# Score tiles in seven PSUM banks taken in pairs, and later layer norms cut into pieces on four engines

## The chip, the cores and the metric

One NeuronCore of a Trainium2 chip runs the whole program. Its engines are TensorE (PE in the profile), VectorE (DVE), ScalarE (ACT), GpSimd (POOL) and SyncE (SP, which here only issues DMAs). Each engine works through its own list of instructions in order and waits on semaphores. The metric is the device time of one execution, in microseconds.

## The reference

The input `x` is `[4, 1024, 128]` in float32. Four blocks follow each other, each added to its own input: a two-layer Mamba block; an encoder layer with a mixture-of-experts attention; then the two attentions that this case is about, and a switch feed-forward.

```python
# L1_attn: 16 heads of width 8, causal, rotary, a distance decay
q_rot, k_rot = _rotate(q, cos, sin), _rotate(k, cos, sin)
scores = einsum('bhqd,bhkd->bhqk', q_rot, k_rot) / sqrt(8) + decay_bias
attn = softmax(where(causal, scores, -inf)); out = (attn @ v) @ Wo.T
# L1_ffn: a second attention, not causal, then eight experts
hn = layernorm(x, ln1_g, ln1_b)
q, k, v = hn @ wq + bq, hn @ wk + bk, hn @ wv + bv      # 16 heads of width 8
x1 = x + (softmax(q @ k.T / sqrt(8)) @ v) @ wo + bo
hn2 = layernorm(x1, ln2_g, ln2_b)
y = x1 + w2[idx] @ relu(w1[idx] @ hn2 + b1[idx]) + b2[idx], idx = argmax(hn2 @ gate_w + gate_b)
```

`L1_attn` is applied to `layernorm(x)`, and `L1_ffn` to `layernorm` of its result, so a batch of the second attention needs two layer norms one after the other.

## The kernel before

The program has four phases with a barrier after each: `Mamba`, `SwitchHead`, `NarrowAttentions`, `MoeFfn`. The change is in the third.

**Sources and units.** A source is one batch of one attention: sources 0 to 3 are the causal attention's batches, 4 to 7 the other's (`NB` = 4). Each source makes two units of 8 heads, so there are 16 units, 0 to 7 causal and 8 to 15 not. Within a unit, `hp` is a pair of heads, `t` one of 8 tiles of 128 tokens and `q` one of two halves of 512 tokens.

**Steps.** For each (`hp`, `t`, `q`) a unit has a `row` and a `col`. A `row` step is two matmuls (one for each head, line 2253) into a pair of PSUM banks, and a maximum over them on VectorE (line 2418). A `col` step is two matmuls of the transposed scores (line 2271) into a pair of banks, with the row maximum already subtracted by three extra contraction rows, and one exp on ScalarE (line 2357) into the SBUF tile `P`. Causal tiles on the diagonal add masking matmuls (lines 2258, 2276). A `values` step multiplies one `t` of `P` with the values into the accumulator bank `OB` (line 2300). After 8 of these ScalarE copies the bank out (`copy`, line 2364), TensorE transposes it (`finish`, line 2227) and VectorE divides by the sums (lines 2438, 2445). When a unit's rows are done, `max_mm` and `max_t` bring the maxima into place through TensorE, ScalarE and six small DMAs. A causal unit has 48 rows and 48 cols, another 64 and 64.

**The order** is one list of steps, made by `order`, which every engine goes through and takes its own parts of. The rows of unit n+1 are dealt among the cols of unit n, nearly one for one; in the last unit there are only cols, and before unit 0 only rows. `after` adds `values`, `copy` and, two cols later, `finish`; `out_t` and `out` (the output projection, one per source) follow in the next unit. A side sequence `source(s)` prepares source s during unit 2s-3 (source 1 during unit 0's rows): one of its steps follows every third col. Its steps are `norm` (and `norm2` for s >= 4), `rows` (8 transposes, ScalarE copies them to `XT`), for each of two sides `qk`, (`qk2`), `hi`, `mid`, `lo`, and at last `v`. `experts_first` does the same for the first expert batch (`g_norm`, `g_rows`) in unit 15.

**The norms** are whole on VectorE (`layer_norm`): 8 bn_stats, 8 bn_aggr, a wait for ScalarE's square root (`row_root`, line 198, between two loads of an activation table), five small operations, 8 tensor_scalars (line 204), and with a gain two broadcast tensor_tensors (lines 2485, 2487).

**PSUM.** Banks 0 to 5 are a ring, `Banks(..., c.ps, 6, ...)`, in which every use takes 2 neighbouring banks; banks 6 and 7 are the two `OB`. A use waits on TensorE (`empty`) until the reader of the last use of its banks is done; the reader waits for `full`.

## Time and profile before

| | us |
|---|---|
| median of 3 runs (lowest, highest) | 6000.66 (5996.47, 6005.03) |
| the profiled execution: its own time | 6004.54 |
| its span in the profile | 6002.8 |
| the phase `NarrowAttentions` in it | 3948 to 5505 |
| unit 13 (not causal, no source beside it) | 95.2 |
| unit 9 (not causal, with source 6) | 121.8 |

A unit is read here from the copy of its predecessor's last `OB` to that of its own last `OB`. PE busy time counts pipelined matmuls and their modelled ends, so a busy PE can still be waiting for a bank.

### The profile page before, as it was taken

The page shows a single profiled execution, that of the slowest core. Times are in us where ns is not written, and L with a number is a line of the kernel's source. Part 1 is how long each engine was busy: PE and PEld are TensorE (multiplying, and loading weights), DVE is VectorE, ACT ScalarE, POOL GpSimd, SP SyncE. Part 2 cuts the span into 40 slices and gives each one's busy share as a digit, 9 for nine tenths or more (in the row PEclk, how much of TensorE's full clock was granted, in tenths as well). Part 3 has the DMA queues.
Part 4 walks back from the last instruction along what each step waited for, and adds up shares of the span by engine and source line. Part 5 has one row for each costly group of instructions (what it writes and reads, how often), then busy time and mean ns, then how long its engine had stood idle before and what let it go on. Part 6 is the DMA issues. An engine that isn't in the chain of part 4 may idle for free. (4 is left out here: it accounts for less than half of the span.)

```text
span 6002.8 us, 73017 instructions
## 1 busy us (share of the span) xinstructions
PE 5422.2 (90%) x25792; PEld 2257.1 (38%) x25792; DVE 4262.6 (71%) x4735; ACT 2550.3 (42%) x2902; POOL 2487.9 (41%) x1169
## 2 busy tenths in 40 slices
PE   7988987799999999999999999968888787887999
PEld 2333333233333334333433343333332222222777
DVE  6999898877777776777677767576667878871222
ACT  5655563232223233222332323225555666675332
POOL 4888887566555655556555556510000000000000
PEclk9999999899999999999999999979998999998999
DMA  4555554010101010101101100122111100101000
GB/s 148 187 183 185 181 190 160 20 41 20 35 21 31 20 41 23 31 20 37 27 20 34 40 20 26 35 47 39 36 28 28 28 22 22 23 1 30 4 4 8
DMA packets 133557, 314.62 MB, mean 52 GB/s; under 512 B 29644, under 2 KB 50516, under 8 KB 132916
## 3 DMA queue, kind: packets, MB, share of 16 engines
q1 hardware_dynamic: 133208, 309.96, 17.7%
q8 instruction: 220, 3.60, 0.2%
q14 instruction: 129, 1.06, 0.1%
HBM read 268.05 MB, written 23.86 MB: 49 GB/s over the span
## 5 line engine op out<-in xcount | busy, mean ns | idle before, releaser
L2418 DVE TENSOR_REDUCE n_MX<-ps 128x2 f32<-128x1024 f32 (+1 forms) x896 | 972.5, 1107 | 250.2 <-PE ps L2253 166.8
L1962 POOL TENSOR_TENSOR s_PA<-s_PA,shared 128x1024 f32<-128x1024 f32 x384 | 908.9, 2367 | 318.6 <-ACT shared L1538 290.7
L2357 ACT ACTIVATE n_P<-ps 128x1024 f32<-128x1024 f32 (+2 forms) x896 | 816.0, 932 | 448.2 <-PE ps L2271 227.3
L1538 ACT ACTIVATE shared<-ps 128x1024 f32<-128x1024 f32 x512 | 522.6, 1023 | 1127.3 <-PE ps L1372 1115.1
L766 POOL TENSOR_TENSOR m_PR<-m_HH,m_CS 128x1024 f32<-128x1024 f32 x256 | 606.0, 2383 | 162.1 <-issue 146.5
L1704 DVE TENSOR_REDUCE s_MX<-ps 128x2 f32<-128x1024 f32 x512 | 592.5, 1200 | 5.8 <-PE ps L1355 5.5
L1696 DVE TENSOR_TENSOR XTB<-ps,s_GVJ 128x1024 f32<-128x1024 f32 x256 | 312.8, 1222 | 358.4 <-PE ps L1346 356.4
L1355 PE MATMUL ps<-s_QF 64*128 64x512 f32 x2048 | 501.9, 607 | 71.2 <-DVE XTB L1696 44.8
L1368 PE MATMUL ps<-s_QF 64*128 64x512 f32 x2048 | 554.1, 617 | 6.6 <-DVE s_MX L1704 4.7
L2300 PE MATMUL ps<-n_P,n_VA 128*32 128x512 f32 (+3 forms) x3584 | 529.6, 590 | 18.7 <-ACT n_P L2357 18.3
L543 PE MATMUL ps<-m_PR,ident 128*128 128x512 f32 x1024 | 505.7, 621 | 11.1 <-DVE m_ZS L735 6.6
L1410 PE MATMUL ps<-s_OG,s_WO 128*128 128x512 f32 x1024 | 501.8, 612 | 0.7 <-DVE s_OUTT L1746 0.5
L1383 PE MATMUL ps<-shared,s_V 128*64 128x512 f32 x2048 | 499.0, 608 | 0.0
L1346 PE MATMUL ps<-s_WV,XTB 128*128 128x512 f32 x1024 | 482.8, 594 | 1.3 <-DVE XTB L1696 0.8
L729 DVE TENSOR_TENSOR_SCAN m_HH<-m_DA,ps 128x1024 f32<-128x1024 f32 x176 | 402.4, 2286 | 6.6 <-ACT m_DA L665 0.6
L1733 DVE TENSOR_TENSOR s_OG<-ps,s_OT 128x1024 f32<-128x1024 f32 x256 | 310.8, 1214 | 90.8 <-issue 61.1
L1924 POOL TENSOR_TENSOR s_TA<-s_TA,s_CS 128x1024 f32<-128x1024 f32 x64 | 151.3, 2365 | 475.4 <-DMA s_TA<-XTB 475.4
L2496 POOL TENSOR_TENSOR XTB<-XTB,n_PT 128x1024 f32<-128x1024 f32 x14 | 29.8, 2132 | 719.0 <-ACT n_PT L2330 708.7
L1698 DVE TENSOR_REDUCE s_V<-XTB 128x128 f32<-128x1024 f32 x256 | 312.3, 1220 | 8.8
L1355 PEld LDWEIGHTS ps<-s_QF 64*128 64x128 f32 x2048 | 200.9, 190 | 304.2 <-issue 274.5
L1410 PEld LDWEIGHTS ps<-s_OG,s_WO 128*128 128x128 f32 x1024 | 178.1, 189 | 307.9 <-issue 306.3
L1368 PEld LDWEIGHTS ps<-s_QF 64*128 64x128 f32 x2048 | 177.2, 186 | 290.4 <-issue 284.8
(344 smaller groups left out, 7816.2 us busy)
## 6 DMA issues: line engine op xcount, KB each, us to landing
m_CS<-m_rows_c SPq DMA_DIRECT2D x256, 512.0 KB, 3.7
m_BS<-m_rows_c SPq DMA_DIRECT2D x80, 512.0 KB, 5.0
s_WV<-in_s_v SPq DMA_DIRECT2D x32, 512.0 KB, 3.6
s_TA<-XTB SPq DMA_DIRECT2D x256, 64.0 KB, 2.3
s_WO<-in_s_o SPq DMA_DIRECT2D x32, 512.0 KB, 4.0
n_parts<-n_PT SPq DMA_DIRECT2D x14, 768.0 KB, 3.3
shared<-n_parts SPq DMA_DIRECT2D x144, 64.0 KB
n_QS<-n_parts SPq DMA_DIRECT2D x120, 64.0 KB
```

The costliest lines, as they stand in the source:

```text
L543: ins = pe.matmul(self.PY[:, q], c.ident[:, :], self.PR[n % 4][:, q], start=j == 0, stop=j == self.NS - 1)
L766: g.tensor_tensor(self.PR[n % 4][:, :], self.HH[n % 4][:, :], self.CS[n % self.NCS][:, :], ALU.mult).then_inc(self.prod_done, 1)
L1355: ins = pe.matmul(ps[:, 512 * h:512 * h + 512], QF[hs, 0, t * 128:(t + 1) * 128], QF[hs, 1, 512 * q:512 * q + 512], start=True, stop=True)
L1368: pe.matmul(ps[:, 512 * h:512 * h + 512], QF[hs, 1, t * 128:(t + 1) * 128], QF[hs, 0, qs], start=True, stop=False)
L1383: ins = pe.matmul(self.O[64 * h:64 * h + 64, :], self.V[j % 2][:, h, t, :], self.P[g % 4][:, 512 * h:512 * h + 512], start=t == 0, stop=t ...
L1410: ins = pe.matmul(self.Z, self.WO[j % 2][:, 2 * e + i, :], self.OG[e % 2][:, i, :], start=e == i == 0, stop=e == 3 and i == 1)
L1538: s.activation(self.P[g % 4], ps, ACT.Exp).then_inc(*r.take(step))
L1704: v.tensor_reduce(self.MX[:, q, :, t], ps.rearrange("p (h n) -> p h n", h=2), AX.X, ALU.max, negate=True).then_inc(*r.take(step))
L1962: g.tensor_tensor(PA, PA, P, ALU.add).then_inc(self.add_done, 1)
L2300: ins = pe.matmul(ob[at:at + 32, lo - 512 * q:512], self.VA[s % 3][:, t, 8 * g + 2 * hp + hh, :], self.P[(32 * n + 8 * hp + t) % 3][q][:, ...
L2357: s.activation(self.P[(32 * n + 8 * hp + t) % 3][q][:, :, lo:512], ps.rearrange("p (h n) -> p h n", h=2)[:, :, lo:512], ACT.Exp, scale=sca ...
L2418: v.tensor_reduce(self.MX[:, q, :, hp, t], ps.rearrange("p (h n) -> p h n", h=2)[:, :, 0:width], AX.X, ALU.max).then_inc(*r.take(step))
```

## The change

A new class `Pairs` replaces `Banks` for this phase: it has seven banks, and use k takes the next two, going round, so that one use in seven has bank 6 and bank 0. A use that needs one access pattern over both (`apart` false: all but `row` and `col`) skips bank 6 instead. A `row` or `col` on the pair (6, 0) is read by two instructions, one for each bank. One bank, 7, is left for `OB`.

The norms become four steps: `norm` (the statistics, VectorE), `norm_root` (ScalarE), `norm_scale` (six small operations, VectorE) and `norm_out` (8 activations, ScalarE). The gain after `norm2` and `g_norm` is a step of its own on GpSimd, and so is the last bias of `out` for sources 4 to 7. Each step still follows a third col, or a second one in units 5 and 7. Left out of the diff: renamed semaphores, an unchanged copy of `Banks`' methods, and that the steps' counts follow.

```diff
+class Pairs:
+    def __init__(self, nc, ctx, name, PS, n, uses):
+        self.full = ctx.enter_context(nc.semaphore(f"{name}_full"))
+        self.read = {e: ctx.enter_context(nc.semaphore(f"{name}_read_{e}")) for e in "vs"}
+        self.q, self.place, self.before, self.reader, self.turn = {}, {}, {}, {}, {}
+        at, count, seen = 0, {"v": 0, "s": 0}, [{"v": 0, "s": 0} for _ in range(n)]
+        banks = PS[:, 0:512 * n].rearrange("p (b n) -> p b n", b=n)
+        for k, (step, apart, reader) in enumerate(uses):
+            if at == n - 1 and not apart:
+                at = 0
+            two = sorted((at, (at + 1) % n))
+            mine = [seen[b] for b in two]
+            self.before[step] = {e: max(m[e] for m in mine) for e in "vs"}
+            count[reader] += 1
+            for m in mine:
+                m[reader] = count[reader]
+            if not apart:
+                self.q[step] = PS[:, 512 * at:512 * at + 1024]
+            elif two[1] - two[0] == 1:
+                self.q[step] = [banks[:, two[0]:two[0] + 2, :]]
+            else:
+                self.q[step] = [banks[:, b:b + 1, :] for b in two]
+            self.place[step], self.reader[step], self.turn[step] = k + 1, reader, count[reader]
+            at = (at + 2) % n
+    def half(self, step, h):
+        return self.q[step][0][:, h, :] if len(self.q[step]) == 1 else self.q[step][h][:, 0, :]
...
-        self.OB = [c.ps[:, 3072:3584], c.ps[:, 3584:4096]]
+        self.OB = c.ps[:, 3584:4096]
-        self.r = Banks(nc, ctx, "n_psum", c.ps, 6, [(s, 2, who(s)) for s in self.steps if s[0] in engine or s[0] == "qk"])
+        self.r = Pairs(nc, ctx, "n_psum", c.ps, 7, [(s, s[0] in ("row", "col"), who(s)) for s in self.steps if s[0] in engine or s[0] == "qk"])
...
     def source(self, s):
         out = self.out
-        out.append(("norm", s))
-        yield
+        yield from self.norm_pieces("norm", s)
         if s >= NB:
-            out.append(("norm2", s))
+            yield from self.norm_pieces("norm2", s)
+            out.append(("gain", s))
             yield
...
     def experts_first(self):
-        for kind in ("g_norm", "g_rows"):
+        yield from self.norm_pieces("g_norm", 0)
+        for kind in ("g_gain", "g_rows"):
             self.out.append((kind, 0))
             yield
+    def norm_pieces(self, kind, s):
+        for k in (kind, kind + "_root", kind + "_scale", kind + "_out"):
+            self.out.append((k, s))
+            yield
...
-            cols = list(self.cols(n))
+            cols, apart = list(self.cols(n)), 2 if n < 8 and s >= NB else 3
-                if i % 3 == 2:
+                if i % apart == apart - 1:
...
-                pe.wait_ge(self.norm_done, n)
+                if n < NB:
+                    pe.wait_ge(self.ln_out, self.ln("norm", n))
+                else:
+                    pe.wait_ge(self.gain_done, n - NB + 1)
...
-            if 4 * n + hp >= 2:
-                pe.wait_ge(self.oc_done, 4 * n + hp - 1)
+            if 4 * n + hp > 0:
+                pe.wait_ge(self.oc_done, 4 * n + hp)
...
-                s.activation(self.P[(32 * n + 8 * hp + t) % 3][q][:, :, lo:512], ps.rearrange("p (h n) -> p h n", h=2)[:, :, lo:512],
-                             ACT.Exp, scale=scale).then_inc(*r.take(step))
+                P, at = self.P[(32 * n + 8 * hp + t) % 3][q], 0
+                for x in ps:
+                    ins = s.activation(P[:, at:at + x.shape[1], lo:512], x[:, :, lo:512], ACT.Exp, scale=scale)
+                    at += x.shape[1]
+                ins.then_inc(*r.take(step))
...
             if kind in ("norm", "norm2", "g_norm"):
-                self.layer_norm(v, own, step)
+                if self.ln(*step) > 1:
+                    v.wait_ge(self.ln_out, self.ln(*step) - 1)
+                if kind == "g_norm":
+                    v.wait_ge(self.y_done, 1)
+                stats_sums(c, v, own, self.norm_source(kind, n), self.norm[step])
+            elif kind in ("norm_scale", "norm2_scale", "g_norm_scale"):
+                stats_scale(c, v, own, self.norm[kind[:-6], n], (self.ln_chain, 1))
...
-                v.tensor_reduce(self.MX[:, q, :, hp, t], ps.rearrange("p (h n) -> p h n", h=2)[:, :, 0:width], AX.X,
-                                ALU.max).then_inc(*r.take(step))
+                at = 0
+                for x in ps:
+                    ins = v.tensor_reduce(self.MX[:, q, at:at + x.shape[1], hp, t], x[:, :, 0:width], AX.X, ALU.max)
+                    at += x.shape[1]
+                ins.then_inc(*r.take(step))
...
-                r.taken(v, step)
-                if n >= NB:
-                    v.tensor_tensor(dst, dst, self.lnp[:, 3, :].unsqueeze(1).to_broadcast([128, NT, 128]),
-                                    ALU.add).then_inc(self.y_done, 1)
...
+    def norm_out(self, s, kind, n):
+        c, r = self.c, self.r
+        src = self.norm_source(kind, n)
+        dst = self.norm_source("norm2", n) if kind == "norm" and n >= NB else self.XN
+        s.wait_ge(self.ln_chain, self.ln(kind, n))
+        if kind == "norm" and n == NB + 1:
+            s.wait_ge(self.va0_done, 1)
+        elif kind == "norm" and n == NB + 2:
+            for side in range(2):
+                r.taken(s, ("qk", NB - 1, side))
+                r.taken(s, ("qk2", NB - 1, side))
+        if dst is self.XN:
+            before = self.S if kind == "g_norm" else n
+            if before > 1:
+                r.filled(s, ("rows", before - 1))
+        for i in range(NT):
+            ins = s.activation(dst[:, i, :], src[:, i, :], ACT.Identity, scale=c.rs[:, 6, i:i + 1],
+                               bias=c.rs[:, 7, i:i + 1])
+        ins.then_inc(self.ln_out, 1)
...
+            if kind in ("gain", "g_gain"):
+                XN, t = self.XN[:, :, :], self.lnp if kind == "gain" else self.glnp
+                g.wait_ge(self.ln_out, self.ln("norm2" if kind == "gain" else "g_norm", n))
+                g.wait_ge(self.consts_in, 16 * 4)
+                g.tensor_tensor(XN, XN, row(t, 0), ALU.mult).then_inc(*own.up())
+                own.wait()
+                g.tensor_tensor(XN, XN, row(t, 1), ALU.add).then_inc(self.gain_done, 1)
+            elif kind == "out" and n >= NB:
+                dst = c.Y[:, (n - NB) * NT:(n - NB + 1) * NT, :]
+                r.taken(g, step)
+                g.tensor_tensor(dst, dst, row(self.lnp, 3), ALU.add).then_inc(self.y_done, 1)
```

## Rows read from the trace of the kernel before

**Rows 1.** Page, busy time and share of the span of one engine

```profile
PE 5422.2 (90%) x25792; PEld 2257.1 (38%) x25792; DVE 4262.6 (71%) x4735; ACT 2550.3 (42%) x2902; POOL 2487.9 (41%) x1169
```

**Rows 2.** Windows (stretch, length; PE, PEld, DVE, ACT, POOL busy; clock): phase, units 6, 9, 13

```profile
3948.00:5500.00 1552.00, 1245.14 (x9920) 418.50 (x9920) 1136.07 (x1651) 960.81 (x1125) 84.96 (x40) 0.91 0.13 26
4502.18:4575.15 72.97, 65.60 (x651) 25.54 (x649) 52.47 (x68) 42.65 (x58) 0.00 (x0) 0.95 0.14 24
4778.35:4900.11 121.76, 88.91 (x563) 24.86 (x561) 94.86 (x153) 81.04 (x88) 8.55 (x4) 0.89 0.11 27
5221.25:5316.47 95.22, 78.35 (x531) 19.41 (x529) 79.69 (x83) 67.10 (x72) 0.00 (x0) 0.95 0.10 18
```

**Rows 3.** Timeline, one round of the steady pattern, unit 12: start, us, engine, line

```profile
5165.27 0.39 PE L2271 MATMUL ps<-shared 51*128 51x512 bf16 x2
5165.70 3.00 ACT L2357 ACTIVATE n_P<-ps 128x1024 f32<-128x1024 f32 x3 [0.51 <-PE ps L2271]
...
5166.86 0.39 PE L2253 MATMUL ps<-n_KS,n_QS 48*128 48x512 bf16 x2 [0.77 <-ACT n_P L2357]
...
5167.30 3.68 DVE L2418 TENSOR_REDUCE n_MX<-ps 128x2 f32<-128x1024 f32 x3 [0.16 <-PE ps L2253]
...
5168.10 1.06 PE L2300 MATMUL ps<-n_P,n_VA 128*32 128x512 f32 x8
...
5169.53 1.02 ACT L2357 ACTIVATE n_P<-ps 128x1024 f32<-128x1024 f32 x1 [0.83 <-PE ps L2271]
...
5170.64 0.39 PE L2271 MATMUL ps<-shared 51*128 51x512 bf16 x2
```

**Rows 4.** Groups of instructions by form: exps, and maxima of units 5 to 14

```profile
L2357 ACT ACTIVATE n_P<-ps 128x1024 f32<-128x1024 f32 x704 | 702.0, 1023 | 288.3 <-PE ps L2271 227.3 <-PE ps L2276 52.9
L2357 ACT ACTIVATE n_P<-ps 128x512 f32<-128x512 f32 x64 | 38.2, 598 | 70.3 <-PE ps L2276 70.3
...
L2418 DVE TENSOR_REDUCE n_MX<-ps 128x2 f32<-128x512 f32 x12 | 8.3, 693 | 5.5 <-PE ps L2258 5.2
```

**Rows 5.** Timeline, the norms of source 6 in unit 9

```profile
4782.72 1.64 DVE L176 BATCH_NORM_STATS2 ln_stats<-X 128x6 f32<-128x128 f32 x8
4783.05 1.28 ACT L198 ACT_TABLE_LOAD   x1
...
4786.56 2.14 DVE L204 TENSOR_SCALAR Y<-X,ln_mean_var,ln_small 128x128 f32<-128x128 f32 x8
...
4792.27 1.63 DVE L176 BATCH_NORM_STATS2 ln_stats<-Y 128x6 f32<-128x128 f32 x8
...
4799.34 1.23 DVE L2485 TENSOR_TENSOR n_XN<-n_XN,n_lnp 128x1024 f32<-128x1024 f32 x1
...
4803.06 0.61 PE L2271 MATMUL ps<-shared 51*128 51x512 bf16 x2 [7.74 <-DVE n_MX L2418]
```

**Rows 6.** Windows: first quarters of units 9 and 13, and 4 us after a stall

```profile
4778.35:4822.90 44.55, 27.13 (x152) 7.73 (x150) 35.12 (x84) 26.24 (x27) 2.14 (x1) 0.77 0.20 35
5221.25:5247.93 26.68, 22.08 (x140) 5.22 (x138) 21.91 (x22) 17.61 (x18) 0.00 (x0) 0.87 0.34 58
...
4790.00:4794.00 4.00, 3.94 (x18) 0.74 (x18) 3.92 (x11) 1.48 (x2) 0.00 (x0) 0.50 0.55 98
```

**Rows 7.** Timeline of VectorE: first and last of nine maxima beside ScalarE's parts

```profile
4839.37 1.23 DVE L2418 TENSOR_REDUCE n_MX<-ps 128x2 f32<-128x1024 f32 x1 [0.31 <-PE ps L2253]
...
4851.37 1.23 DVE L2418 TENSOR_REDUCE n_MX<-ps 128x2 f32<-128x1024 f32 x1 [0.31 <-PE ps L2253]
```

**Rows 8.** Timeline, ScalarE's scale-and-bias activations in the phase before

```profile
3944.64 1.65 ACT L1482 ACTIVATE s_XN<-s_XN,ln_small 128x128 f32<-128x128 f32 x4 [2.91 <-DVE ln_small L810]
```

**Rows 9.** Page, the costliest groups: a GpSimd tensor_tensor on float32

```profile
L1962 POOL TENSOR_TENSOR s_PA<-s_PA,shared 128x1024 f32<-128x1024 f32 x384 | 908.9, 2367 | 318.6 <-ACT shared L1538 290.7
```

**Rows 10.** Timeline, the norm of source 1, ahead of unit 0

```profile
3956.53 2.50 DVE L189 TENSOR_SCALAR ln_small<-ln_small 128x8 f32<-128x8 f32 x1
...
3962.50 1.94 PE L2190 MATMUL ps<-ident,n_XN 128*128 128x128 f32 x8 [8.97 <-DVE n_MX L2418]
```

More of the change, by code:

```diff
@@ L86, in __init__, with ap, empty, filled @@
             at += width
+    def ap(self, step):
+        return self.q[step]
+    def empty(self, e, step):
+        for reader, count in self.before[step].items():
+            if count:
+                e.wait_ge(self.read[reader], count)
+    def filled(self, e, step):
+        e.wait_ge(self.full, self.place[step])
+    def taken(self, e, step):
+        e.wait_ge(self.read[self.reader[step]], self.turn[step])
+    def fill(self, step):
+        return self.full, 1
+    def take(self, step):
+        return self.read[self.reader[step]], 1
+class Pairs:
[24 more added lines that the diff above has]
+        return self.q[step][0][:, h, :] if len(self.q[step]) == 1 else self.q[step][h][:, 0, :]
     def ap(self, step):
@@ L2252, in row @@
             hs = slice(64 * hh, 64 * hh + k)
-            ins = pe.matmul(ps[:, 512 * hh:512 * hh + width], Q[hs, hp, t * 128:(t + 1) * 128],
+            ins = pe.matmul(self.r.half(step, hh)[:, 0:width], Q[hs, hp, t * 128:(t + 1) * 128],
                             K[hs, hp, 512 * q:512 * q + width], start=True, stop=not diag)
@@ L2256, in row @@
             for hh in range(2):
-                hs, end = slice(64 * hh, 64 * hh + 64), 512 * hh + width
-                ins = pe.matmul(ps[:, end - 128:end], self.EM[hs, a, :], self.EM[hs, 2 + a, :], start=False, stop=a == 1)
+                hs = slice(64 * hh, 64 * hh + 64)
+                ins = pe.matmul(self.r.half(step, hh)[:, width - 128:width], self.EM[hs, a, :], self.EM[hs, 2 + a, :], start=False, stop=a == 1)
         ins.then_inc(*self.r.fill(step))
@@ L2270, in col @@
             hs = slice(64 * hh, 64 * hh + k)
-            ins = pe.matmul(ps[:, 512 * hh + lo - 512 * q:512 * hh + 512], K[hs, hp, t * 128:(t + 1) * 128],
+            ins = pe.matmul(self.r.half(step, hh)[:, lo - 512 * q:512], K[hs, hp, t * 128:(t + 1) * 128],
                             Q[hs, hp, lo:512 * q + 512], start=True, stop=not diag)
@@ L2274, in col @@
             for hh in range(2):
-                hs, at = slice(64 * hh, 64 * hh + 64), 512 * hh + lo - 512 * q
-                ins = pe.matmul(ps[:, at:at + 128], self.EM[hs, a, :], self.EM[hs, 4 + a, :], start=False, stop=a == 1)
+                hs, at = slice(64 * hh, 64 * hh + 64), lo - 512 * q
+                ins = pe.matmul(self.r.half(step, hh)[:, at:at + 128], self.EM[hs, a, :], self.EM[hs, 4 + a, :], start=False, stop=a == 1)
         ins.then_inc(*self.r.fill(step))
@@ L2309, in scalar @@
             ps = r.ap(step) if step in r.q else None
-            if kind in ("norm", "norm2", "g_norm"):
-                row_root(c, s, self.norm[step])
+            if kind in ("norm_root", "norm2_root", "g_norm_root"):
+                row_root(c, s, self.norm[kind[:-5], n])
+            elif kind in ("norm_out", "norm2_out", "g_norm_out"):
+                self.norm_out(s, kind[:-4], n)
             elif kind in ("rows", "g_rows"):
@@ L2451, in vector @@
                 v.tensor_tensor(flat(dst), flat(dst), ps, ALU.add).then_inc(*r.take(step))
-                r.taken(v, step)
-                if n >= NB:
-                    v.tensor_tensor(dst, dst, self.lnp[:, 3, :].unsqueeze(1).to_broadcast([128, NT, 128]),
-                                    ALU.add).then_inc(self.y_done, 1)
         c.own_count = own.n
-    def layer_norm(self, v, own, step):
-        c, n = self.c, step[1]
-        if step[0] == "norm" and n < NB:
-            if n > 1:
-                self.r.filled(v, ("rows", n - 1))
-            row_stats(c, v, own, c.batch(n), self.norm[step])
-            normalize(c, v, own, c.batch(n), self.XN, (self.norm_done, 1))
-            return
-        first = step[0] == "g_norm"
-        Yb = c.Y[:, 0:NT, :] if first else c.Y[:, (n - NB) * NT:(n - NB + 1) * NT, :]
-        if first:
-            v.wait_ge(self.y_done, 1)
-        if step[0] == "norm":
-            if n == NB + 2:
-                for side in range(2):
-                    self.r.taken(v, ("qk", NB - 1, side))
-                    self.r.taken(v, ("qk2", NB - 1, side))
-            row_stats(c, v, own, c.batch(n - NB), self.norm[step])
-            normalize(c, v, own, c.batch(n - NB), Yb)
-            own.wait()
-            return
-        v.wait_ge(self.consts_in, 16 * 4)
-        gain = lambda i: (self.glnp if first else self.lnp)[:, i, :].unsqueeze(1).to_broadcast([128, NT, 128])
-        row_stats(c, v, own, Yb, self.norm[step])
-        self.r.filled(v, ("rows", self.S - 1 if first else n - 1))
-        normalize(c, v, own, Yb, self.XN)
-        own.wait()
-        v.tensor_tensor(self.XN[:, :, :], self.XN[:, :, :], gain(0), ALU.mult).then_inc(*own.up())
-        own.wait()
-        v.tensor_tensor(self.XN[:, :, :], self.XN[:, :, :], gain(1), ALU.add).then_inc(self.norm_done, 1)
@@ new lines, in norm_source @@
+    def norm_source(self, kind, n):
+        return self.c.batch(n % NB) if kind == "norm" else self.c.Y[:, n % NB * NT:(n % NB + 1) * NT, :]
+    def norm_out(self, s, kind, n):
[17 more added lines that the diff above has]
+        ins.then_inc(self.ln_out, 1)
@@ L2502, in gpsimd @@
     def gpsimd(self, g):
-        r = self.r
+        c, r = self.c, self.r
+        own = Own(g, self.own_gain)
+        row = lambda t, i: t[:, i, :].unsqueeze(1).to_broadcast([128, NT, 128])
         for u in range(3):
```

18 lines of the change are left out of this document (11 added, 7 removed).

## The prediction

> **What bounds the kernel now.** The page comes first: TensorE is busy for 90% of the span [rows 1]. The change touches only the third phase, 1557 us of it, so the windows come next. There no engine is full: TensorE 80%, VectorE 73%, ScalarE 62% [rows 2]. Such a phase is bound by a loop of waits, and the timeline shows which. In the steady pattern of a non-causal unit a round of 4 rows, 4 cols and 2 values steps takes 5.37 us [rows 3]: a col is filled at 5165.27, its exp starts at 5165.70, the next exp follows back to back and ends at about 5167.7; that frees the banks of the row at 5167.78; the values step starts at 5168.10, then a col, a row and a second values step, and the next round's col fills at 5170.64. Two exps and two values steps in series are the loop. VectorE is beside it with 4 x 1.227 = 4.9 us of work, ScalarE with 4.0 us and gaps of 0.51 and 0.83.
>
> The ring closes this loop: it has 3 slots, so use k waits for the reader of use k-3; the row at 5166.86 waited 0.77 us for an exp [rows 3]. Anything put on VectorE or ScalarE stops the others within three uses. Unit 9 with its source takes 121.8 us, unit 13 without one 95.2 [rows 2]. The first quarters show where: 44.55 against 26.68, so 17.9 us go in the quarter with both norms [rows 6]. VectorE is blocked there from 4782.72 to 4788.70 and from 4792.27 to 4801.8, 6.0 and 9.5 us [rows 5]; TensorE idles for up to 7.7 us, and the granted clock after the first stall is 0.50, the lower level, 1.2 GHz [rows 6].
>
> **Seven banks.** I go through the ring's rule use by use. With pairs (0,1) (2,3) (4,5) (6,0) (1,2) (3,4) (5,6), use k always holds one bank of use k-3, and the other is of k-3 or k-4. `empty` waits for both before the first matmul, so the wait is for use k-3, as with six banks; a skipped bank 6 leads to the same. Over the list's 1923 uses I count no steady use that could start a use earlier. The gain is 0: the seventh bank holds half a tile that nobody can start on. If I were wrong and a row or col could start one use earlier, the loop would open until VectorE bounds it at 1.23 a row in place of 1.34; that is a rival below.
>
> What it costs: 143 rows and 123 cols fall on (6,0) and are read by two instructions. A maximum over half the width takes 0.693 [rows 4], so two take 1.39 against 1.23: +0.16 each, 22 us of VectorE in all. Two exps of 0.598 take 1.20 against 1.023 [rows 4]: +0.17 alone; three full ones in a row take 3.00 and not 3.07 [rows 3], so I take 0.14, 17 us of ScalarE. Of this VectorE's part mostly fits in its 0.47 us of idle time a round; it counts ahead of unit 0, where only rows run: 7 x 0.16 = 1. Of the exps two in four are in the loop: 8. Sum +9; bounds 4 and 39. The Trainium skill (ScalarE: Activation LUTs, What ACT_TABLE_LOAD costs) has back-to-back activations overlap by 93 ns, twice or more what these rows show; by it a wrapped col costs 0.08 and the term is 6.
>
> One `OB`: values of t = 0 now wait for the copy just before. In the list `finish`, which waits on TensorE for that same copy, stands ahead of that values step for every head pair. It is the cover, and the cost is 0. Without it each of 63 copies would add up to its 0.6 us.
>
> **Norms in pieces: the price of a piece.** ScalarE's gaps let me work out what an insertion of X costs the loop: before the second exp of a back-to-back pair all of X, before the others X - 1.1 or nothing. The mean for 1.05 us is 0.53. The trace tests it: 8 intervals of maxima beside two such pieces take 12.00 us [rows 7] against 8 x 1.34 = 10.8, so 0.6 for each. On VectorE I let an insertion lose 0.8 (its idle 0.47 a round and the lead of its readers; between 0.5 and 1.1). By this the two blocks cost 15.5 - 1.6 = 13.9, the lower clock some 2, and 2 are left of the 17.9 for transposes and copies, which fits.
>
> Before, for a norm with its stall: VectorE 6.0 (statistics 2.5, wait and small operations 1.35, normalize 2.14), with ScalarE's root hidden in it. After, four insertions:
> - statistics, VectorE 2.5: costs 1.7
> - root, ScalarE, table load 1.28 [rows 5], sqrt 0.2, load back 1.28, together 2.77, now with nothing beside it that waits anyway: (2.77 + 1.67)/2 = 2.2
> - scale, VectorE, five small operations and a sixth, 1.2: 0.4
> - out, ScalarE: four such activations take 1.65 [rows 8], so 8 take 3.3, against VectorE's 2.14 for the same: (3.3 + 2.2)/2 = 2.75
>
> Together 7.05, 14.1 for two norms. The gain's two tensor_tensors (1.23 each [rows 5]) leave VectorE for GpSimd, 2 x 2.37 [rows 9]. `rows` waits for them on TensorE, with all later steps behind it; but six cols, over 8 us, lie between `norm2_out` and `rows`, against 3.3 + 4.75 from ScalarE's start. In units 5 and 7 only four do, and I count 1.4 us of stall for each.
>
> **The sum**, against the profiled 6004.5:
> - wrapped pairs +9
> - sources 6 and 7: 14.1 + 0.5 of clock against 13.9 + 2: -1.3, taken -1.5 each; sources 4 and 5, in causal units with more idle time (VectorE 72% in unit 6 [rows 2]), -1 each with the stall: together -5
> - sources 2 and 3: one norm, 7.05 less the causal slack against 5.2 and half a clock fall: 0
> - source 1: only rows run, so the exposed work is VectorE's. TensorE idled 8.97 [rows 10]; 8.8 of VectorE become 4.3, and `rows` waits some 1.5 for ScalarE: -3
> - the first expert norm, in unit 15 where ScalarE is the bound: about 8 us lost before, and 2.77 + 3.3 + a copy of 1.02 and 1 us of waiting for GpSimd after: 0
> - three biases of `out` leave VectorE: 3 x -1.2 = -3.5; the fourth is the phase's last work, 1.23 becomes 2.37 and a semaphore: +1.3
>
> Sum: 9 - 5 - 3 - 3.5 + 1.3 = -1.2, so 6003.3 for the profiled execution. It stands 3.9 above the median of the runs, so the forecast is 5999. For this kernel 0.2% is 12 us; less can't be told from no change.
>
> **Rivals.**
> - *Faster: pieces hide.* If every ScalarE piece costs half its length, as 1.05 us did [rows 7], a norm costs 3.0 + 2.1 = 5.1. Four sources give 10.2 - 15.9 = -5.7 each, sources 2 and 3 -1 each: 25 us in all with the other terms, 5976. For it: the two pieces that cost 0.6 each. Against it: the pieces are three times as long as the gaps. 0.24.
> - *Faster: the seventh bank opens the loop.* 512 non-causal pairs x 0.11 = 56 us, 5945. The wait for k-3 speaks against it. 0.03.
> - *Slower: the second instruction of a wrapped pair is in the path every time.* Place: each use of (6,0). Price: 22 + 17 = 39 in place of 9, so 6029. For it: every reader frees a slot that someone waits for within three uses; against it, the two loop exps of four. It decides once more than 22 of the 39 us are exposed. 0.17.
> - *Slower: no piece is absorbed.* A norm costs 3.7 + 6.07 = 9.8; against the blocks at full length this is +18 over the forecast, 6017. 0.08.
> - *Slower: GpSimd holds VectorE up.* A tensor_scalar on 8 columns took 2.50 us while GpSimd's memset ran, against 0.17 elsewhere [rows 10]; 14 new GpSimd operations x 2.37 would be 33 us, 6032. Maxima of PSUM beside GpSimd work kept their 1.23, so only a small operation can be caught. 0.03. The Trainium skill (SBUF — State Buffer, Who interferes with whom) says the same of both kinds: the port pair is locked for a whole instruction, and a tensor_reduce never asks for it. The trace agrees with its 2.50 and 1.23.
> - *The forecast:* 0.45, by itself 5989 to 6013.
>
> Range: from the hidden pieces to most of the wrapped pairs' price, 5975 to 6025. Faster 0.27, within 0.2% 0.45, slower 0.28.
>
> **What would show it.** Quarters of unit 13, with no source: 22.19 before; 22.3 to 22.5 if the ring gains nothing and the wraps cost half, 22.7 and more if all, under 21.5 if the loop opened. TensorE's wait of 0.77 on an exp must still be in the steady round. Unit 9's first two quarters: the pieces as four stalls of 1.5 to 3 us in place of two of 5.5 and 7.7, and a clock above 0.77. ScalarE's total rises by 12 x 3.3 + 17 = 57 us; VectorE's falls by 12 x 2.14 + 14 x 1.23 - 22 - 2 = 19. GpSimd's rises by 33. The forecast is wrong if units without a source move by more than 1 us, or if unit 9 moves by more than 4.

## The result, and the profile after

The changed kernel is slower by 0.3%: its median is 6019.99 us (7 runs, 6017.60 to 6025.88) against 6001.19 for the kernel before in the same sitting (7 runs, 5996.47 to 6006.16), a ratio of 1.0031 [1.0021, 1.0041]. The forecast was 5999 and no measurable change. The profiled execution of the changed kernel took 6025.88 with a span of 6024.1.

The page's line of busy time, to be read against [rows 1]:

```profile
PE 5443.6 (90%) x25754; PEld 2258.0 (37%) x25792; DVE 4235.6 (70%) x4782; ACT 2590.1 (43%) x3122; POOL 2520.1 (42%) x1183
```

VectorE lost 27 us of work, ScalarE gained 40, GpSimd 32: the work moved about as the diff says, and all of it was done. The time is lost elsewhere. The windows of the same stretches as in [rows 2]: the phase, then units 6, 9, 13.

```profile
3948.00:5513.76 1565.76, 1264.09 (x9908) 417.30 (x9908) 1109.52 (x1696) 1000.75 (x1344) 115.46 (x53) 0.91 0.12 26
4499.56:4572.23 72.67, 64.87 (x683) 26.71 (x683) 51.86 (x78) 43.91 (x66) 0.00 (x0) 0.99 0.11 24
4782.53:4913.46 130.93, 99.19 (x563) 25.49 (x561) 89.54 (x144) 87.32 (x115) 13.23 (x6) 0.83 0.10 25
5238.34:5333.90 95.56, 78.64 (x533) 19.44 (x529) 80.34 (x93) 67.51 (x81) 0.00 (x0) 0.95 0.12 18
```

Units 6 and 13, beside which no source is prepared, are where they were (72.97 and 95.22 before). Unit 9, with source 6, went from 121.76 to 130.93, though VectorE has 5.3 us less to do in it; ScalarE has 6.3 more and the granted clock fell from 0.89 to 0.83. All units, in us from copy to copy (unit 0 from 3948):

| unit | 0 | 1 | 2 | 3 | 4 | 5 | 6 | 7 |
|---|---|---|---|---|---|---|---|---|
| before | 145.8 | 84.8 | 71.7 | 85.9 | 71.7 | 94.4 | 73.0 | 108.2 |
| after | 142.5 | 91.3 | 72.1 | 91.4 | 72.2 | 96.2 | 72.7 | 101.0 |

| unit | 8 | 9 | 10 | 11 | 12 | 13 | 14 | 15 |
|---|---|---|---|---|---|---|---|---|
| before | 95.0 | 121.8 | 101.9 | 121.6 | 97.7 | 95.2 | 97.6 | 82.6 |
| after | 95.3 | 130.9 | 96.5 | 132.2 | 96.5 | 95.6 | 96.5 | 83.1 |

The last accumulator is copied at 5496.57 before and at 5513.76 after, so 17.2 of the two spans' 21.3 us arise in these units. Units 9, 11, 1 and 3 lose 9.2, 10.7, 6.5 and 5.5; units 7, 10 and 0 win 7.2, 5.4 and 3.3. Of the other 4 us, 1.2 is the last bias, now 2.34 on GpSimd; 2.9 lie in the last phase, which the change doesn't touch.

Where in unit 9? Its four quarters, each from one copy of `OB` to the next:

```profile
4782.53:4818.78 36.25, 24.85 (x140) 5.66 (x138) 27.75 (x64) 23.38 (x33) 0.00 (x0) 0.78 0.24 43
4818.78:4852.47 33.69, 25.91 (x146) 6.58 (x144) 20.58 (x27) 24.52 (x34) 4.72 (x2) 0.84 0.00 0
4852.47:4881.10 28.63, 23.79 (x138) 6.15 (x137) 19.85 (x22) 21.13 (x27) 5.21 (x3) 0.88 0.07 28
4881.10:4913.46 32.36, 24.64 (x145) 7.10 (x145) 21.36 (x33) 18.29 (x23) 3.31 (x2) 0.84 0.08 28
```

Before they took 44.55 [rows 6], 28.59, 24.49 and 24.13. The first two quarters, which hold both norms, together win 3.2 us. The third loses 4.1 and the last 8.2, and no piece of a norm runs in the last. The timeline of the last quarter shows what does:

```profile
4884.54 2.12 POOL L2575 TENSOR_TENSOR XTB<-XTB,n_PT 128x1024 f32<-128x1024 f32 x1 [2.25 <-ACT n_PT L2404]
4885.26 1.49 DVE L2510 TENSOR_TENSOR n_MM<-n_MX 128x64 f32<-128x64 f32 x1
...
4886.80 0.30 PE L2287 MATMUL ps<-ident,n_MM 128*64 128x128 f32 x1 [2.22 <-DVE n_MM L2510]
...
4889.11 1.93 PE L2369 MATMUL ps<-n_P,n_VA 128*32 128x512 f32 x8
...
4897.42 2.36 PE L2279 MATMUL ps<-n_wf,XTB 128*128 128x128 f32 x16
4897.53 1.02 ACT L2430 ACTIVATE n_P<-ps 128x1024 f32<-128x1024 f32 x1 [2.21 <-PE ps L2340]
...
4899.82 1.68 DVE L2491 TENSOR_TENSOR n_VA<-ps,n_lnp 128x128 f32<-128x128 f32 x8 [3.47 <-PE ps L2279]
```

The source's last steps (the residues on GpSimd at line 2575, that is, what is left of `XTB` when a bf16 piece is taken off, and the matmuls and additions of `v` at 2279 and 2491) now fall together with `max_mm` and `max_t` of the next unit (2510, 2287). The source has 19 steps in place of 12, still one after every third col, so it ends behind col 57 of the unit's 64 and not behind col 36. After the 2.22 us in which TensorE waited, a values step takes 1.93 in place of 1.06: the clock is at its lower level, 1.2 GHz, again.

The pieces in the first quarter look as the prediction drew them, with both table loads between exps and TensorE waiting behind them:

```profile
4793.84 1.28 ACT L253 ACT_TABLE_LOAD   x1
...
4795.14 0.21 ACT L253 ACTIVATE ln_small<-ln_small 128x8 f32<-128x8 f32 x1
4795.36 1.28 ACT L2430 ACT_TABLE_LOAD   x1
4796.65 1.94 ACT L2430 ACTIVATE n_P<-ps 128x1024 f32<-128x1024 f32 x2
4797.82 0.61 PE L2322 MATMUL ps<-n_KS,n_QS 48*128 48x512 bf16 x2 [2.65 <-ACT n_P L2430]
...
4806.20 3.18 ACT L2560 ACTIVATE Y<-X,ln_small 128x128 f32<-128x128 f32 x8
```

And the steady round of unit 12, against [rows 3]: the row still waits 0.77 for an exp, and a wrapped col is two instructions of 1.09 together.

```profile
5185.41 1.09 ACT L2430 ACTIVATE n_P<-ps 128x512 f32<-128x512 f32 x2 [0.84 <-PE ps L2340]
...
5186.95 3.00 ACT L2430 ACTIVATE n_P<-ps 128x1024 f32<-128x1024 f32 x3 [0.45 <-PE ps L2340]
...
5188.11 0.39 PE L2322 MATMUL ps<-n_KS,n_QS 48*128 48x512 bf16 x2 [0.77 <-ACT n_P L2430]
```

### The profile page after: what moved, and what is told of

The parts are those of the page before. It is cut to its first block and busy times, and to the rows that moved or that the text cites. A ratio compares the mean times of both kernels' runs of the same rounds, so it can differ in the third digit from the quotient of the medians.

```text
span 6024.1 us, 73273 instructions
## 1 busy us (share of the span) xinstructions
PE 5443.6 (90%) x25754; PEld 2258.0 (37%) x25792; DVE 4235.6 (70%) x4782; ACT 2590.1 (43%) x3122; POOL 2520.1 (42%) x1183
## 5 line engine op out<-in xcount | busy, mean ns | idle before, releaser
L2502 DVE TENSOR_REDUCE n_MX<-ps 128x2 f32<-128x1024 f32 (+7 forms) x1041 | 981.2, 974 | 289.5 <-PE ps L2322 187.9
L2430 ACT ACTIVATE n_P<-ps 128x1024 f32<-128x1024 f32 (+3 forms) x1020 | 821.2, 839 | 434.5 <-PE ps L2340 230.1
L2369 PE MATMUL ps<-n_P,n_VA 128*32 128x512 f32 (+3 forms) x3584 | 545.0, 608 | 20.6 <-ACT n_P L2430 20.4
L784 DVE TENSOR_TENSOR_SCAN m_HH<-m_DA,ps 128x1024 f32<-128x1024 f32 x176 | 402.5, 2287 | 6.6 <-ACT m_DA L720 0.6
L2322 PE MATMUL ps<-n_KS,n_QS 48*128 48x512 bf16 (+2 forms) x1120 | 215.7, 378 | 86.6 <-ACT n_P L2430 64.2
```

Source lines behind the costliest of these rows:

```text
L2369: ins = pe.matmul(ob[at:at + 32, lo - 512 * q:512], self.VA[s % 3][:, t, 8 * g + 2 * hp + hh, :], self.P[(32 * n + 8 * hp + t) % 3][q][:, ...
L2430: ins = s.activation(P[:, at:at + x.shape[1], lo:512], x[:, :, lo:512], ACT.Exp, scale=scale)
L2502: ins = v.tensor_reduce(self.MX[:, q, at:at + x.shape[1], hp, t], x[:, :, 0:width], AX.X, ALU.max)
```

## The experiments

All kernels are the changed one with these switches (for the kernel before, every part is switched back):

```diff
+RING, OBN = 7, 1      # banks of the ring, accumulator banks
+SPREAD = {...}        # norms cut into pieces; the others' parts stand together in the order, as before
+OUT_S = SPREAD        # norms whose 8 scale-and-bias operations run on ScalarE
+GAIN_G = {4, 5, 6, 7, 0}; BIAS_G = {4, 5, 6, 7}      # gains, last biases on GpSimd
+LATE_APART = 3        # cols from one side step to the next in units 9 and 11
```

| kernel | median | ratio to before | unit 9 | unit 11 | units 1, 3 |
|---|---|---|---|---|---|
| before | | | 121.8 | 121.6 | 84.8, 85.9 |
| after | 6019.99 | 1.0031 [1.0021, 1.0041] | 130.9 | 132.2 | 91.3, 91.4 |
| r7_only | 6009.32 | 1.0007 [0.9999, 1.0016] | 119.6 | 119.6 | 86.7, 85.4 |
| r7_halves | 6027.88 | 1.0043 [1.0029, 1.0057] | 124.2 | 122.3 | 87.3, 87.2 |
| norms_only | 6010.76 | 1.0018 [1.0009, 1.0026] | 130.7 | 132.5 | 91.1, 89.0 |
| gains_only | 5981.50 | 0.9967 [0.9955, 0.9979] | 120.6 | 120.0 | 84.8, 86.0 |
| norms_warm | 6019.38 | 1.0028 [1.0020, 1.0037] | 128.3 | 126.6 | 91.1, 88.9 |
| gains_warm | 5990.63 | 0.9980 [0.9971, 0.9989] | 124.4 | 120.1 | 84.9, 86.0 |
| spread_v | 6010.54 | 1.0012 [1.0003, 1.0021] | 127.7 | 129.1 | 88.9, 90.4 |
| whole_s | 6007.55 | 1.0005 [0.9997, 1.0014] | 121.0 | 124.1 | 86.7, 88.4 |
| norms_noload | 5985.94 | 0.9972 [0.9961, 0.9982] | 119.0 | 119.3 | 89.3, 88.0 |
| gains_noload | 5987.27 | 0.9974 [0.9965, 0.9983] | 120.6 | 118.6 | 84.8, 85.0 |
| norms_early | 5983.11 | 0.9967 [0.9955, 0.9980] | 118.8 | 118.0 | 91.1, 88.9 |
| after_early | 5995.33 | 0.9986 [0.9977, 0.9995] | 118.9 | 118.6 | 91.3, 91.4 |
| gains_late | 5992.61 | 0.9982 [0.9973, 0.9991] | 121.5 | 124.3 | 86.1, 84.9 |
| early_all | 6000.56 | 0.9993 [0.9985, 1.0002] | 119.0 | 118.8 | 95.6, 95.6 |
| mix | 5980.52 | 0.9964 [0.9950, 0.9978] | 123.1 | 120.0 | 86.0, 84.9 |
| early_best | 5983.85 | 0.9967 [0.9955, 0.9979] | 118.8 | 118.7 | 86.0, 84.9 |

### The ring alone, and the norms alone

**r7_only**: seven banks and one `OB`, all norms, gains and biases as before.

```diff
-SPREAD, GAIN_G, BIAS_G = {...}, {4, 5, 6, 7, 0}, {4, 5, 6, 7}
+SPREAD, GAIN_G, BIAS_G = set(), set(), set()
```

> The change's seven-bank pairs and single OB alone, with the norms whole on VectorE as before. Theory A (the ring gains no depth; the wrapped pairs' second instruction costs 0.3 to 0.5 us in a unit): slower than before by 3 to 8 us, quarters without a source 22.3 us against 22.19, and most of the change's 19 us lies elsewhere. Theory B (the wrapped pairs are the loss): slower by 15 us or more. If the ring did gain depth: faster, quarters under 22.

**norms_only**: the change without its ring.

```diff
-RING, OBN = 7, 1
+RING, OBN = 6, 1
```

> The change's norms, gains and biases with a ring of six banks (bank 6 unused, single OB). Theory A: slower than before by 11 to 16 us, units 9 and 11 each by 8 to 11, units 1 and 3 by 5 to 6, unit 7 and the stretch ahead of unit 0 shorter by 7 and 3. Theory B: within 4 us of before.

**gains_only**: of the change, only the gains and the last biases on GpSimd.

```diff
-RING, OBN, SPREAD = 7, 1, {...}
+RING, OBN, SPREAD = 6, 2, set()
```

> Before, with only the gains of norm2 and g_norm and the last bias of out moved to GpSimd; norms whole on VectorE, six banks, two OB. If what GpSimd takes is off VectorE's block and hidden by the cols ahead of rows: faster than before by 8 to 16 us. If rows now waits for GpSimd (4.7 us in place of 2.5, with only three cols between norm2 and rows): no faster than 3 us, with TensorE waiting at the transposes.

By its ratio r7_only loses some 4 us to the ring and the single `OB`, with an interval from nothing to 10. Two pairs of kernels differ in the ring alone: norms_only and the changed kernel, and norms_early and after_early (below). By their ratios the ring costs 8 and 11 us there, each give or take 8 or 9; all three readings together allow 4 as well as 10. A quarter of unit 13 with nothing beside it takes 22.19 with six banks and 22.25 to 22.32 with seven: no depth is gained, and little is paid. In units 9 and 11 the loss stays with the norms: norms_only has them as long as the changed kernel to 0.3 us. Moving the gains and biases alone wins 0.33%, some 20 us, more than was expected and more than the 14 instructions of 1.23 us that leave VectorE; of it 4.0 us are in unit 13, in whose code nothing is changed. There the clock goes with it; its first quarter and whole, in gains_only, against [rows 6] and [rows 2]:

```profile
5203.48:5227.41 23.93, 19.33 (x140) 5.11 (x138) 21.82 (x22) 17.60 (x18) 0.00 (x0) 1.00 0.31 66
5203.48:5294.72 91.24, 74.10 (x531) 19.44 (x529) 79.42 (x83) 66.82 (x72) 0.00 (x0) 1.00 0.09 19
```

VectorE's and ScalarE's work are the same to 0.3 us; the clock is 1.00 in place of 0.95. So the same unit is 91.2 or 95.2 long as the clock stands in it, above all behind the unit boundary, where 2.75 of the 4.0 us are, and differences of 4 us in a unit without a source prove nothing about its code. Unit 0, whose code is the same in the changed kernel and in after_early, took 142.5 and 137.4.

**r7_halves**: r7_only, where each of a pair's two matmuls waits for its own bank, the earlier free one first. It tests whether the odd bank can be used at all.

```diff
-        self.r.empty(pe, step)
-        for hh in range(2):
+        for hh in self.r.order(step):
+            self.r.empty_half(pe, step, hh)
```

> As r7_only, but row and col wait for each bank by itself, the earlier free one first, so that the seventh bank lets one of the two matmuls start a use earlier. If TensorE's fill were what the ring waits for: undisturbed quarters under 22.0 us against 22.25 and 22.32 in r7_only. My theory (the other matmul still waits for the reader of use k-3, and the reader needs both): 22.1 to 22.6, no faster.

It is slower by 0.4%; quarters without a source take 22.7 to 24.4. A first half that is written earlier helps nobody, since the reader waits for both. Why it is slower than r7_only no run separates.

### The clock

Both kernels add matmuls that nobody reads, into the bank that six banks and one `OB` leave free, to keep TensorE at work where it would wait for a norm. **norms_warm** is norms_only with 9 of them behind the statistics, the root and the output of each norm of sources 4 to 7; **gains_warm** is gains_only with one `OB` and 20 behind each statistics step of these sources.

```diff
+            if kind == "warm":
+                for _ in range(WARM):
+                    pe.matmul(c.ps[:, 3072:3584], self.EM[0:64, 0, :], self.EM[0:64, 0:4, :], start=True, stop=True)
```

> As norms_only, and TensorE multiplies nine times a constant tile of 512 columns into the unused bank 6 (results not read) three scores after the statistics, the root and the output of each norm of sources 4 to 7, to fill the stalls. Clock theory (each of the eight stalls per source drops TensorE to the 1.2 GHz level for some 3 us, and the values steps at 1.9 instead of 1.06 us are the loss): values steps at 1.06 in unit 9, granted clock above 0.92 there, and units 9 and 11 shorter than in norms_only by 3 to 6 us each. Serial theory (the pieces' own lengths on ScalarE are the loss, the clock is a by-product): the same or longer than norms_only, by up to 2 us for each source.

> As gains_only with one OB, and TensorE multiplies twenty times a constant tile of 512 columns into the unused bank 6 (results not read) three scores after each of the two statistics of sources 4 to 7, which fills most of the 5.5 us stalls. Clock theory: the values steps after the stalls take 1.06 and not 1.9 us, units 9 and 11 shorter by 2 to 4 us each than in gains_only. Serial theory: within 1 us.

In norms_warm the clock of units 9 and 11 rose from 0.83 and 0.82 to 0.89 and 0.91, and they took 2.3 and 5.9 us less; units 5 and 7 took 5.1 and 4.0 more, and the whole was slower. In gains_warm units 7 and 9 took 2.8 and 3.8 more than in gains_only, units 5 and 11 the same to 0.4. The clock carries a part of the loss, but this remedy costs as much as it gives, and how large the part is stays open.

### Which part of a norm costs when it is spread

**spread_v**: all norms in pieces, their eight scale-and-bias operations on VectorE.

```diff
-RING, OBN = 7, 1
+RING, OBN = 6, 2
 SPREAD = {...}
-OUT_S = SPREAD
+OUT_S = set()
```

> As gains_only, but each norm in four pieces with cols between, normalize still on VectorE. Serial theory (a piece stops the ring for about its own length, so what spreading costs is the root's 2.77 us, which VectorE's block hid before): units 9 and 11 at 125 to 127 us against 120 in gains_only and 131 in norms_only, unit 1 at 88 to 90 against 85. Rival (the loss is ScalarE's slower normalize, 3.2 for 2.1 us): units 9 and 11 at 119 to 122.

**whole_s**: gains_only, with the eight operations on ScalarE, all parts of a norm still together.

```diff
-OUT_S = set()
+OUT_S = {("norm", s) for s in range(1, 8)} | {("g_norm", 0)}
```

> As gains_only, each norm's steps together, but normalize on ScalarE. Serial theory: statistics to scale 3.9 us on VectorE and then 3.2 on ScalarE, 1.1 more than VectorE's 6.0 for each norm: units 9 and 11 at 121 to 124. Rival (ScalarE's part is most of the loss): 127 or more.

**norms_noload** and **gains_noload**: norms_only and gains_only, where a copy stands for the square root, so that no table is loaded.

```diff
-                row_root(c, s, self.norm[kind[:-5], n])
+                s.wait_ge(c.var_done, self.norm[kind[:-5], n])
+                s.activation(c.rs[:, 1, :], c.rs[:, 0, :], ACT.Copy).then_inc(c.root_done, 1)
```

> As norms_only, but the root of each norm of the third phase is a copy on ScalarE in place of the square root (so the output is not the reference's), and both table loads go. Serial theory: with the pieces spread, the 2.6 us of table loads stop the ring for their length: units 9 and 11 shorter than in norms_only (131 and 133) by 5 to 8 us each with the clock, unit 1 by 2 to 3. Rival (what spreading costs is the number of stalls, not their length): 1 to 3 us each.

> As gains_only, with the same copy in place of the square root (the output is not the reference's). Serial theory: VectorE's block hides the table loads but for its wait of 0.3 and 1.3 us, so units 9 and 11 are shorter than in gains_only (120.6 and 120.0) by 1 to 3 us each only. Rival: as much as in norms_noload, 5 us or more.

Putting the eight operations on VectorE wins 3 us in each of units 9 and 11, and 7 to 9 of the loss remain. In one piece whole_s adds 0.4 and 4.1 there. So the place of the eight operations is not what makes units 9 and 11 long. Over the whole it is not cheap, though: whole_s has lost all that gains_only had won, by the ratios some 23 us, of which units 1, 3, 5, 7 and 11 show 1.9, 2.4, 3.8, 4.7 and 4.1 (and unit 13, whose code it doesn't touch, 4.8). The table loads are a stronger term. Spread out, they are worth 11.7 and 13.2 us in units 9 and 11, more than the 4 x 1.28 of their own time; in one piece they are worth 0 and 1.4. The timeline of gains_only shows why that is so little: the load runs while VectorE computes the statistics, and the root waits only 0.94.

```profile
4777.45 1.63 DVE L843 BATCH_NORM_STATS2 ln_stats<-X 128x6 f32<-128x128 f32 x8
...
4777.78 1.28 ACT L253 ACT_TABLE_LOAD   x1
...
4780.00 0.21 ACT L253 ACTIVATE ln_small<-ln_small 128x8 f32<-128x8 f32 x1 [0.94 <-DVE ln_small L848]
```

But in units 1 and 3 the loads are worth only 1.9 and 1.0 of the 6.4 and 3.1 that spreading costs there, and in unit 9 they pay in quarters in which there is no load: its last falls from 32.36 to 29.2. The loads are an amplifier; something else makes the last quarter long. Yet without them units 9 and 11 are back at 119.0 and 119.3, though the source still ends behind col 57 and the last quarter is still long: taking out the loads wins as much as the late end costs.

### How far apart the side steps stand

**after_early**: the changed kernel, whole, but for one number: in units 9 and 11 a side step follows every second col, so the source ends behind col 38 and not 57. **norms_early** is norms_only with the same number.

```diff
-LATE_APART = 3
+LATE_APART = 2
```

> The changed kernel itself, ring of seven and all, with one number changed: in units 9 and 11 a side step follows every second col and not every third. If the late end of the source beside max_mm and max_t is what the change lost: last quarters at 23 to 25 us in place of 32.4, units 9 and 11 at 118 to 122, in all 18 to 28 us faster than the change and 3 to 10 faster than before. If the seven banks matter for it: still slower than before.

> As norms_only, but in units 9 and 11 too a side step follows every second col, so that a source ends at col 38 and not at col 57 of 64. If part of the loss is that hi, mid, lo and v of the second side now fall together with max_mm and max_t in the last quarter (32.4 us there against 24.1): the last quarter back at 24, units 9 and 11 shorter by 4 us or more. If it only moves the same stalls: within 2 us of norms_only, the last quarter shorter and the others longer.

In after_early this takes 12.1 and 13.6 us out of units 9 and 11 of the changed kernel and turns its ratio from 1.0031 to 0.9986. Unit 9 as a whole, then its first and its last quarter:

```profile
4777.45:4896.32 118.87, 90.99 (x563) 24.85 (x561) 88.40 (x147) 87.20 (x114) 13.24 (x6) 0.90 0.11 28
4777.45:4813.28 35.83, 23.92 (x140) 5.45 (x136) 28.55 (x70) 28.92 (x44) 0.73 (x1) 0.86 0.23 44
...
4873.34:4896.32 22.98, 17.84 (x129) 4.88 (x128) 18.35 (x24) 16.56 (x24) 0.00 (x0) 1.00 0.02 4
```

VectorE's and ScalarE's work in the unit is within 1.2 us of that in the changed kernel. The last quarter is 22.98 where it was 32.36, at full clock; GpSimd is idle in it. The norms' own first quarter did not grow (35.83 against 36.25).

**gains_late** makes the coincidence without the pieces: gains_only with a side step after every fifth col of units 9 and 11, so that the source ends behind col 60.

```diff
-LATE_APART = 3
+LATE_APART = 5
```

> As gains_only, with whole norms on VectorE, but in units 9 and 11 a side step follows every fifth col, so that the same twelve steps end at col 59 of 64. If the coincidence with the unit's end is a cost of its own, without any piece: last quarters at 30 us or more against 25.1, units 9 and 11 longer than 120.6 and 120.0 by 4 to 9 us. If the pieces are the cost: within 2 us.

The last quarters grow from 25.1 to 27.3 and 28.2, units 9 and 11 by 0.9 and 4.3, and the whole by some 9 us. The lateness alone costs, but a third or less of what it costs beside the pieces. (A last quarter of 30 us or more was expected.) The same quarter of unit 9 before, in gains_late and in norms_noload, to be read against the 32.36 at a clock of 0.84 above:

```profile
4875.98:4900.11 24.13, 19.29 (x129) 4.71 (x128) 18.41 (x22) 16.61 (x21) 0.00 (x0) 0.93 0.02 4
...
4867.79:4895.08 27.29, 21.71 (x145) 6.59 (x144) 20.25 (x30) 18.42 (x22) 2.12 (x1) 0.94 0.09 32
...
4859.23:4888.43 29.20, 21.55 (x145) 6.70 (x144) 21.17 (x30) 18.39 (x22) 3.25 (x2) 0.94 0.09 31
```

At a like clock a late source makes it 3.2 us longer, and 1.9 more where the norms are in pieces. norms_noload has the wait of 2.2 us for `n_MM` too; the last 3.2 us, from 29.20 to 32.36, come with the lower clock. These kernels differ in more than one thing, so this is a reading of the 8.2 us and not a proof.

One difference is to be seen in the steps themselves, `n_MM` of all 16 units, first in the changed kernel, then in gains_only:

```profile
L2510 DVE TENSOR_TENSOR n_MM<-n_MX x16: 224/226/1927, 4010.7 to 5425.0; 128x64 f32<-128x64 f32 x16
```

```profile
L2561 DVE TENSOR_TENSOR n_MM<-n_MX x16: 224/225/226, 4014.2 to 5385.5; 128x64 f32<-128x64 f32 x16
```

In the changed kernel it takes 1.49 in units 9 and 11, 1.93 in unit 5, 0.48 in units 1 and 3, and 0.22 elsewhere; in gains_late 0.58 at most. The long ones run beside GpSimd's residue, as in the timeline above, and `max_mm` is at the head of the chain on which all cols of the next unit wait. In units 1 and 3 the residue catches the next link of this chain, in `max_t`, which takes 0.27 elsewhere:

```profile
4158.19 1.81 DVE L2513 TENSOR_TENSOR n_MR<-n_MT,n_M 64x128 f32<-64x128 f32 x1 [0.41 <-ACT n_M L2416]
```

How much of a unit such an instruction makes, no run isolates. It need not be dear: in unit 5 of norms_only `n_MM` takes 1.87 and the unit 91.7, and in gains_only 0.22 and 91.1.

**early_all** is norms_early with a side step after every second col in units 1 and 3 too.

```diff
-... apart = ..., 2 if n < 8 and s >= NB and ("norm", s) in SPREAD else 3 if n < 8 or n == 15 else LATE_APART
+... apart = ..., 2 if n < 8 and s >= NB and ("norm", s) in SPREAD else 3 if n == 15 else LATE_APART
```

> As norms_early, with every second col in units 1 and 3 as well, where a source of 14 steps ended at col 42 of 48. If the same cause made units 1 and 3 slower (91.1 and 88.9 against 84.8 and 85.9 before): 84 to 87 there. If in those units the pieces themselves cost: still 88 or more.

Units 1 and 3 get worse, 95.6 against 91.1 and 88.9. Unit 1 by quarters: norms_only has 25.7, 22.6, 24.3 and 18.6, early_all 35.0, 23.8, 21.8 and 15.0. The end is freed here as well, by 6.1 us, and `n_MM` and `n_MR` of these units take 0.22 and 0.27 again, but the first quarter, into which the whole norm now falls together with the transposes, pays 9.3. In the causal units with one norm neither spacing wins against the block (84.8 and 85.9).

### Versions put together

**mix**: gains_only, with sources 1 and 5 in pieces and the last bias back on VectorE. **early_best**: sources 1 and 4 to 7 and the expert norm in pieces, side steps after every second col in units 5, 7, 9 and 11, sources 2 and 3 whole on VectorE, the expert norm's eight operations and the last bias on VectorE.

```diff
-RING, OBN, SPREAD, BIAS_G = 7, 1, {("norm", s) for s in range(1, 8)} | {("g_norm", 0)}, {4, 5, 6, 7}
+RING, OBN, SPREAD, BIAS_G = 6, 2, {("norm", 1), ("norm", 4), ("norm", 5), ("norm", 6), ("norm", 7), ("g_norm", 0)}, {4, 5, 6}
-LATE_APART = 3
+LATE_APART = 2
```

> As gains_only, with source 1 (only rows run beside it) and source 5 (in unit 7, 64 rows against 48 cols, VectorE 92 of 108 us busy, ScalarE 56) in four pieces with ScalarE's normalize, and the last bias back on VectorE. If pieces pay only where VectorE alone is the bound: the stretch ahead of unit 0 shorter by 8 to 10 us, unit 7 by 2 to 4, the rest as gains_only, in all 10 to 14 us faster than it. If the gain of unit 0 in norms_only was luck of the clock: within 4 us of gains_only.

> What the runs point to: six banks and two OB; source 1 and sources 4 to 7 in pieces, every second col in units 5, 7, 9 and 11; sources 2 and 3 whole on VectorE; the first expert norm in pieces with normalize on VectorE; gains on GpSimd, the phase's last bias on VectorE. By the sum of the best units seen (139 + 85 + 72 + 86 + 71 + 92 + 71 + 102 + 95 + 119 + 96 + 118 + 95 + 93 + 96 + 81) the phase ends near 5459 against 5476 in gains_only: 35 us faster than before, 20 to 40 with the clock's luck.

Both beat both kernels, and neither can be told from gains_only or norms_early: 0.9964 to 0.9967 with intervals of 0.0012 to 0.0014 to either side. Both expectations were too high: the sum of the best units seen gave 35 us for early_best, and 20 came. The simplest of them moves 14 instructions to GpSimd and changes nothing else. Beside that the pieces, well spaced, win 1.4 to 2.0 us in each of units 9 and 11 (after_early and norms_early against gains_only), less than a unit moves with the clock.

## Why the prediction was wrong

**The step that failed** is in "Norms in pieces: the price of a piece", with the term "sources 6 and 7: ... taken -1.5 each". It priced each piece where it stands and never asked what the seven added steps do to the steps behind them. That "each step still follows a third col" was in the description of the change; 19 steps of 3 cols end at col 57, and `max_mm` and `max_t` come just there. The two units were +9.2 and +10.7. With the one number of after_early they are -2.9 and -2.9 against before, of which the gains alone make -1.2 and -1.6 (gains_only). So in these two units the pieces' own price, as a sum, was about right, and it is the displacement that costs 12 to 14 us in each. That is shown for pieces with their table loads in them. It is not a cause by itself: without the loads the same late end leaves the units at 119.0 and 119.3, and without the pieces it costs 0.9 and 4.3. How the loss divides between the stretched `n_MM`, the lower clock and the plain overlap is read from unlike kernels above and not shown.

The terms of the sum against the units, in us:

| term | predicted | measured |
|---|---|---|
| wrapped pairs, all units | +9 | +4 with the single `OB`, r7_only; +8 and +11 in the two pairs of kernels |
| sources 6, 7 (units 9, 11) | -3 | +19.9 |
| sources 4, 5 (units 5, 7) | -2 | +1.8, -7.2 |
| sources 2, 3 (units 1, 3) | 0 | +6.5, +5.5 |
| source 1 (unit 0) | -3 | -3.3 |
| expert norm (unit 15) | 0 | +0.5 |
| biases of `out` (units 10, 12, 14) | -3.5 | -5.4, -1.2, -1.1 |
| the last bias | +1.3 | +1.2 |

- **Sources 2 and 3** are a second miss of the same step. A part is the same displacement (14 steps end behind col 42 of 48 in place of 33: unit 1's last two quarters grew by 8.7 while its first shrank by 4.7). Spacing alone doesn't mend it, so here the price of a piece itself was too low: "one norm, 7.05 less the causal slack" is not slack enough.
- **Unit 0**: -3.3 against -3 is in part luck, since its length moves by 5 us between kernels that have the same code there.
- **Wrapped pairs**: right in kind. The instructions were priced too dear: two halves of a maximum take 1.29 against 1.23, not 1.39; two of an exp 1.08 to 1.09, not 1.16. The Trainium skill's overlap of 93 ns (ScalarE: Activation LUTs, What ACT_TABLE_LOAD costs), by which a wrapped col costs an estimated 0.08, was nearer to the measured 0.06 than the 0.14 of the rows. Whether its +6 or the +9 was nearer in time, the three readings of the ring can't tell. 145 rows and 124 cols were wrapped (counted 143 and 123).
- **No depth from the seventh bank**: right. 22.25 to 22.32 a quarter against the 22.3 foretold, and the wait of 0.77 is there.
- **One `OB`**: r7_only allows 10 us at most for ring and `OB` together, and copies without cover were priced at up to 63 x 0.6, so the cover held.
- **ScalarE +57, VectorE -19, GpSimd +33**: +40, -27, +32. Eight activations took 3.18 and not 3.3; the wraps cost less on both engines.
- **Unit 9's first two quarters**: foretold as stalls of 1.5 to 3 and a clock above 0.77. TensorE's longest waits in the unit are 2.9 and 2.7, and the clock is 0.78 and 0.84, in the first quarter hardly above the 0.77. The 3.2 us won there are what the pieces bring; the forecast looked no further.
- **What would make it wrong** was named: unit 9 moved by more than 4.

**The rivals.** "The second instruction of a wrapped pair is in the path every time" gave 6029 and comes nearest in time, by a mechanism that r7_only rules out. "No piece is absorbed", 6017, is nearly the time too; after_early, with every piece in place, speaks against it in units 9 and 11; in units 1 and 3, which stay 3 to 11 us longer than with whole norms at either spacing, it is not refuted. "Pieces hide", 5976 (with its own terms 5980; they add up to 21 us and not to 25): no. "GpSimd holds VectorE up" was given 0.03 because only a small operation could be caught. That was right: it caught one small operation in each of units 9, 11 and 5 and two in units 1 and 3, all in the chain of the maxima. Their own lengthening is 1.3 to 1.8 us a unit, and what it costs behind them is open.

## What to carry to other kernels

When work is cut into more steps of a side sequence whose spacing stays, work out where its last step now falls and what runs there: here that cost 12 to 14 us a unit, where the cutting and the moved gains together had won 3. A table load that stands in a block hides under the statistics before it; cut free, it stands between two exps of a full loop. Measure each part of such a change by itself: of three parts one was worth 20 us, and the others had taken it back and as much again.
